# A transformer block with routed experts on one Trainium2 core: the closing stage by pairs of tiles, the experts' loops written out, two pieces of the shared expert in other banks

## The chip, the cores and the metric

The kernel is one program on one core of a Trainium2 chip. The core has five engines with queues of their own: TensorE (PE in the profile; PEld is its weight load, PEldq and PEq its sequencer), VectorE (DVE), ScalarE (ACT), GpSimd (POOL) and SyncE (SP, which here only issues transfers). They wait for one another through semaphores. The metric is the time of one execution on the device in microseconds (us), lower is better.

## The reference

The input x has 4 sequences of 512 tokens, 256 wide. Everything is float32.

```python
mod = silu(c) @ wmod                       # six vectors for each of the 4 sequences
h = layernorm(x) * (1 + ca) + sa
x = x + ga * attention(h)                  # 16 heads of 16, softmax over 512 keys, times wo
h = layernorm(x) * (1 + cb) + sb
logits = h @ gate_w.T                      # 32 experts, 4 are chosen for a token
out = sigmoid(h @ shared_gate) * (silu(h @ sg.T) * (h @ su.T)) @ sd.T
for e in range(32):                        # an expert: 256 -> 96 (gate and up) -> 256
    out += comb[:, e] * (silu(h @ gate_e.T) * (h @ up_e.T)) @ down_e.T
x = x + gb * out
```

comb holds a token's four normalised router weights and is 0 for the other experts. So 4 x 512 x 4 = 8192 (token, expert) pairs are computed.

## The kernel before, in words

The instructions of every engine are written by hand, engine by engine; no scheduler moves them. The functions have the same names in the blocks of several engines, and a semaphore joins them.

**Attention.** For each sequence in turn: normalise, project, scores, exponentials, values, output projection. Between the matrix products of attention TensorE does the projections of the next sequence and the router of the one before. GpSimd scatters the rows of each sequence into the table `dispatched` in memory, sorted by expert (`dispatch`, L541).

**The shared expert's pieces (class Finish, `finish`).** When attention ends, TensorE computes 30 pieces of the shared expert, two matrix products of 128x512 each (L972; SG is a gate, SU an up-projection) or eight of 128x256 (L966; SD, the down-projection). Piece n lies in bank `2 + n % 4` of a list of six; numbers 2 to 5 of that list are the banks 0 to 3 of PSUM. A bank is claimed when VectorE (or ScalarE) has freed its last piece; VectorE's `shared` reads the pieces in the same order (L1436 for SG behind ScalarE's tanh L652, L1445 for SU, L1448 and L1458 for SD). The last two pieces, 28 and 29, are the gates SG0 and SG1 of the last sequence. `CHAIN` and the `if n == ...` lines in the `finish` of TensorE and VectorE put the last sequence's router between the pieces: output projection behind piece 1, transposes and logits behind 6 and 7, ranks behind 10. VectorE works out the table of tiles (`tile_table`, L1392 to L1415) behind piece 12; TensorE turns it into a row (`table`, L952) behind piece 15, and VectorE packs it (`pack_table`, L1420 to L1427) behind piece 15 too.

**The experts.** The table has 96 tiles of 128 rows, each of one expert, taken in 48 pairs, one pair a slot (r is the slot's number modulo 8, q the slot). SyncE reads a tile's place from the table and loads its rows into one of 8 buffers of `xe` (L457). TensorE's slot q is, from `slots`: `turn_rows` (4 transposes of pair q, L1092, into bank 0 or 1), `widen` (up-projection of pair q-1, 4 products, L1106, into bank 2 or 3), `turn_hidden` (2 transposes of q-2, L1117), `narrow` (down-projection of q-3, 2 products, L1127). The profile counts each float32 product as two matrix instructions. Which expert's weights they use comes from `experts`: a word of the table holds four expert numbers and is read into registers (`value_load`, L1082). `slots` keeps the words that it has read in `es`, and `es` is new for each call, that is for each 8 slots:

```python
def known(r):
    w = r // 2
    if w not in es:
        es[w] = experts(XP // 2 * i + w)
    return es[w][2 * (r % 2):2 * (r % 2) + 2]
```

The first slot of a call asks for the words of pairs q-1, q and q-3, the others for one new word in two slots.
VectorE copies the transposed rows to `xeT` (tile oT, L1579) and multiplies gate, up and router weight (L1586, L1588); ScalarE computes silu (L743) and copies the hidden rows (L760) and the results (L752, to `y_sb`). GpSimd scatters the results into `results`, two indirect transfers a slot (L561). A buffer of `xe` is loaded anew when the results of its pair have landed (semaphores `y_out`). On every engine the first 8 slots are written out and the rest is a hardware loop of 5 turns (on GpSimd 6 turns) of 8 slots; the last three steps of the pipeline follow it as straight code.

**The closing stage.** After the experts TensorE computes ten last pieces of the shared expert (class Late). SyncE loads the results back, 16 tiles of 128 tokens x 4 results x 256 (`comb`, L472). For a tile, VectorE adds the four results with one 512-wide and one 256-wide addition (L1618, L1619), multiplies by the gate vector (L1620) and adds to x (L1622). For the tiles in `BY_PE`, (4, 6, 8, 10, 12, 14), TensorE adds the four results with an identity matrix instead (L1177) and VectorE multiplies out of PSUM (L1614) and adds (L1622). `cuts` says ahead of which tile VectorE takes the late pieces. ScalarE stores each tile when it is done (L783).

## Time and profile before

| what | value |
|---|---|
| timed runs | 596.38 us (median of 3; 596.19, 596.38, 599.55) |
| the profiled execution | 599.47 us; its span, first to last instruction, is 597.7 us |
| busy, whole span | TensorE 560.9 us (94%), weight load 308.7 (52%), VectorE 374.9 (63%), ScalarE 255.3 (43%), GpSimd 206.1 (34%) |
| matrix instructions | 3102 products, 3103 weight loads |
| granted clock of TensorE | 0.979 on average; 1.00 from 172 to 570 us |
| queue that fetches TensorE's code (q8) | 21 packets, 0.34 MB |
| experts' stage | 403 to 550 us |
| closing stage | 550 to 597.7 us |

The profile is of one execution, with the time of each instruction. "Busy" is time in which an engine computes; waits, branches, register steps and the issue of transfers are not busy. In a timeline several instructions of one kind are merged (x4), and the bracket behind a row says how long the engine was idle ahead of it and what ended that ("issue" is an idle time that nothing in the profile explains). 0.24 us of idle between TensorE's weight loads is their normal pace beside long products.

### The profile page before, as it was taken

To read this page: it belongs to the slowest core of one execution; us is meant where nothing else is said; L and a number is where in the kernel's file an instruction comes from. 1 tells how busy PE (TensorE), PEld (TensorE's weight loads), DVE (VectorE), ACT (ScalarE), POOL (GpSimd) and SP (SyncE) were. 2 spreads that over 40 slices of the span, in tenths; PEclk is the share of its full clock that TensorE was granted. 3 is DMA by queue.
4 is the path that set the end of the run, shared out by engine and by line. 5 is a ranking of instruction groups with operands and counts; after the bars stand their busy time and mean duration, and the time that the engine had idled before them with its cause. 6 is when DMAs were issued, how large, how long until landed. Compare 5 with 4: busy or idle time off the path is not lost.

```text
span 597.7 us, 10693 instructions
## 1 busy us (share of the span) xinstructions
PE 560.9 (94%) x3102; PEld 308.7 (52%) x3103; DVE 374.9 (63%) x888; ACT 255.3 (43%) x519; POOL 206.1 (34%) x268
## 2 busy tenths in 40 slices
PE   4989999999999999999999998989998999999983
PEld 3443323233333333333343455638887898988572
DVE  6375577778679786798856469545343443442588
ACT  3112635664866648555568240123333343444000
POOL 6200000000020751207533663722665666667200
PEclk9975999999999999999999999999999999999998
DMA  6133117100221222212100688433544655540592
GB/s 228 40 110 123 27 34 218 34 7 16 68 49 37 80 82 77 44 35 82 62 1 29 222 255 249 136 91 107 157 146 137 180 161 159 166 125 18 209 404 91
DMA packets 44119, 67.18 MB, mean 112 GB/s; under 512 B 9499, under 2 KB 32420, under 8 KB 43692
## 3 DMA queue, kind: packets, MB, share of 16 engines
q1 hardware_dynamic: 31984, 45.62, 26.5%
q0 software_dynamic: 7680, 16.87, 8.1%
q10 hardware_dynamic: 4416, 4.20, 2.1%
q8 instruction: 21, 0.34, 0.3%
q14 instruction: 18, 0.15, 0.1%
HBM read 38.93 MB, written 27.51 MB: 111 GB/s over the span
## 4 chain that ended last, share of the span: by engine, by line
PE 83%; DVE 9%; DMA 2%; issue 2%; SPq 2%; ACT 1%; POOL 0%; ACTq 0%; DVEq 0%; POOLq 0%
PE ps L875 23%; PE ps L888 11%; PE ps L1106 9%; PE ps L972 8%; PE ps L1127 6%; PE ps L824 5%; PE ps L966 4%; PE ps L1092 3%; PE ps L846 3%; PE ps L833 3%; PE ps L901 3%; DVE max_q L1217 2%; PE ps L1117 2%; PE ps L810 2%; PE ps L931 1%
## 5 line engine op out<-in xcount | busy, mean ns | idle before, releaser
L1217 DVE TENSOR_REDUCE max_q<-ps 128x1 f32<-128x512 f32 x256 | 163.7, 684 | 73.6 <-PE ps L846 71.7
L703 ACT ACTIVATE probs<-ps 128x512 f32<-128x512 f32 x256 | 138.0, 596 | 102.1 <-PE ps L875 101.8
L846 PE MATMUL ps<-k_rows,q_rows 31*128 31x512 f32 x512 | 150.1, 681 | 1.1 <-DMA k_rows<-qk_raw 1.1
L875 PE MATMUL ps<-q_rows,k_rows 32*128 32x512 f32 x512 | 146.4, 650 | 0.9 <-DVE max_q L1217 0.9
L561 POOL DMA_INDIRECT results<-y_sb,dest x96 | 94.9, 988 | 70.3 <-ACT y_sb L752 35.2
L875 PEld LDWEIGHTS ps<-q_rows,k_rows 32*128 32x128 f32 x512 | 41.8, 186 | 70.6 <-ACT probs L703 51.1
L1106 PE MATMUL ps<-up_sb,oT 128*128 x384 | 70.8, 327 | 0.9 <-issue 0.7
L888 PE MATMUL ps<-probs,v_ext 128*32 128x512 f32 x512 | 68.2, 605 | 1.1 <-ACT probs L703 1.1
L1106 PEld LDWEIGHTS ps<-up_sb,oT 128*128 128x128 f32 x384 | 61.3, 190 | 1.9 <-issue 1.8
L1579 DVE COPY oT<-ps 128x512 f32<-128x512 f32 x48 | 33.1, 691 | 32.8 <-PE ps L1092 32.8
L1127 PE MATMUL ps<-down_sb,e_hidT 96*128 x192 | 49.8, 382 | 4.0 <-ACT e_hidT L760 4.0
L846 PEld LDWEIGHTS ps<-k_rows,q_rows 31*128 31x128 f32 x512 | 45.6, 193 | 9.8 <-DVE max_q L1217 3.9
L514 POOL TENSOR_TENSOR rstd<-veps,mhalf 128x4 f32<-128x4 f32 x4 | 4.1, 1036 | 133.1 <-DVE veps L1299 131.4
L1586 DVE CAST dest<-xe 128x2 int32<-128x2 f32 x48 | 15.0, 313 | 49.2 <-ACT e_silu L743 45.8
L743 ACT ACTIVATE e_silu<-ps 128x192 f32<-128x192 f32 x48 | 15.8, 330 | 59.5 <-PE ps L1106 59.5
L752 ACT ACTIVATE y_sb<-ps 128x512 f32<-128x512 f32 x48 | 28.7, 597 | 29.4 <-PE ps L1127 26.6
L652 ACT ACTIVATE sh_tanh<-ps 128x512 f32<-128x512 f32 x16 | 9.5, 596 | 68.8 <-PE ps L972 68.8
L1127 PEld LDWEIGHTS ps<-down_sb,e_hidT 96*128 96x128 f32 x192 | 32.6, 190 | 8.0 <-issue 5.4
L888 PEld LDWEIGHTS ps<-probs,v_ext 128*32 128x32 f32 x512 | 10.1, 108 | 50.6 <-issue 34.1
L541 POOL DMA_INDIRECT dispatched<-h_even,slot_i x32 | 31.4, 982 | 9.5 <-POOL h_even L540 9.5
L541 POOL DMA_INDIRECT dispatched<-h_odd,slot_i x32 | 31.3, 978 | 9.1 <-POOL h_odd L540 9.1
L1092 PE MATMUL ps<-ident,xe 128*128 128x128 f32 x192 | 29.1, 273 | 3.5 <-issue 2.0
(181 smaller groups left out, 681.9 us busy)
## 6 DMA issues: line engine op xcount, KB each, us to landing
xe<-dispatched SPq DMA_DIRECT2D x96, 129.0 KB, 2.1
comb<-results SPq DMA_DIRECT2D x16, 512.0 KB, 10.6
up_sb<-in_up SPq DMA_DIRECT2D x12, 512.0 KB, 4.7
dispatched<-pad_rows SPq DMA_DIRECT2D x33, 129.0 KB, 4.0
down_sb<-in_down SPq DMA_DIRECT2D x4, 768.0 KB, 6.7
x<-in_x ACTq DMA_DIRECT2D x4, 512.0 KB, 4.8
q_rows<-qk_raw SPq DMA_DIRECT2D x64, 32.0 KB, 1.9
k_rows<-qk_raw SPq DMA_DIRECT2D x64, 32.0 KB, 1.9
```

The source lines that it names most:

```text
L541: pool.indirect_dma_start(out=xs, out_offset=bass.IndirectOffsetOnAxis(ap=slot_i[:, TOPK * j + k:TOPK * j + k + 1], axis=0), in_=h2[p % 2] ...
L561: pool.indirect_dma_start(out=yk, out_offset=bass.IndirectOffsetOnAxis(ap=dest[:, n:n + 1], axis=0), in_=y_sb[:, n % (2 * YP), :], in_offs ...
L703: act.activation(probs[:, u % 8, :], ps[:, st_bank(t.b, g, u), :], ACT.Exp).then_inc(exp_done, 1)
L846: pe.matmul(ps[:, banks[u % len(banks)], :], q_rows[32 * i:32 * i + ONE, b % 2, g, qt * P:(qt + 1) * P], k_rows[32 * i:32 * i + ONE, b % 2 ...
L875: pe.matmul(ps[:, st_bank(b, g, n), :], k_rows[32 * i:32 * i + 32, b % 2, g, kt * P:(kt + 1) * P], q_rows[32 * i:32 * i + 32, b % 2, g, :] ...
L888: mm = pe.matmul(ps[32 * i:32 * i + 32, O, :], v_ext[:, b % 2, kt, head(g, i), :], probs[:, (4 * kt + i) % 8, :], start=(kt == 0), stop=(k ...
L972: mm = pe.matmul(bank, w[:, k, c * P:(c + 1) * P], h2_columns(s, k), start=(k == 0), stop=(k == KD - 1))
L1092: mm = pe.transpose(ps[:, r % 2, (2 * half + k) * P:(2 * half + k + 1) * P], xe[:, 2 * r + half, k * P:(k + 1) * P], ident[:, :])
L1106: mm = pe.matmul(ps[:, 2 + r % 2, 2 * DM * half:2 * DM * (half + 1)], xeT[:, r % 2, (2 * half + k) * P:(2 * half + k + 1) * P], up_sb[:, b ...
L1127: mm = pe.matmul(ps[:, 6 + r % 2, half * D:(half + 1) * D], e_hidT[:, r % 2, half * P:(half + 1) * P], down_sb[:, bass.ds(es[half] * D, D) ...
L1217: dve.tensor_reduce(max_q[:, g % 2, qt, i:i + 1], ps[:, banks[(16 * g + n) % len(banks)], :], AXX, ALU.max).then_inc(max_done, 1)
L1579: dve.tensor_copy(xeT[:, r % 2, :], ps[:, r % 2, :]).then_inc(t_done, 1)
```

## The change

1. **Table.** `CHAIN` and both `finish` functions move TensorE's `table` and VectorE's `pack_table` from behind piece 15 to behind piece 17. `tile_table` stays behind piece 12.
2. **Banks.** Piece n of Finish lies in bank `2 + (n + 2) % 4`, so every piece moves by two banks. The last two are now in banks 2 and 3, and pieces 26 and 27 in banks 0 and 1.
3. **Loops.** The hardware loops of the experts on all five engines become Python loops: the same slots, written out, with constants where registers were.
4. **Closing stage.** VectorE's loop goes over 8 pairs of tiles with operations twice as wide (the gate vector repeated by a stride of 0), `BY_PE` is (6, 10, 14) and means pairs, TensorE sums two tiles into the halves of one bank, `cuts` has 2 in place of 1, and ScalarE stores 8 pairs.

```diff
--- before.py
+++ after.py
@@ -30,7 +30,7 @@
 YP = 4
 CR = 8
 WP = 6
-BY_PE = (4, 6, 8, 10, 12, 14)
+BY_PE = (6, 10, 14)
 
 
 class Steps:
@@ -119,7 +119,7 @@
 class Finish(Turn):
 
 
-    CHAIN = {1: ("WO0", "WO1"), 6: ("HT0", "HT1"), 7: ("LOG",), 10: ("RANK", "CNT"), 15: ("TAB",)}
+    CHAIN = {1: ("WO0", "WO1"), 6: ("HT0", "HT1"), 7: ("LOG",), 10: ("RANK", "CNT"), 17: ("TAB",)}
 
     def __init__(self, b, used):
         super().__init__(b, {"finish"}, used)
@@ -132,7 +132,7 @@
         self.shared += [f"SG0@{B - 1}", f"SG1@{B - 1}"]
         chain = 0
         for n, name in enumerate(self.shared):
-            self.take(name, 2 + n % 4, used)
+            self.take(name, 2 + (n + 2) % 4, used)
             for own in self.CHAIN.get(n, ()):
                 self.take(own, chain % 2, used)
                 chain += 1
@@ -460,7 +460,7 @@
                 if r == XP - 1:
                     written(sp, fin, f"SU3@{B - 2}")
                 load_pair(r, r)
-            with sp.Fori(1, PAIRS // XP, 1) as i:
+            for i in range(1, PAIRS // XP):
                 for r in range(XP):
 
                     sp.wait_ge(y_out[r % YP], 32 * (XP // YP * (i - 1) + r // YP + 1))
@@ -552,7 +552,7 @@
             scale_and_shift(fin)
             dispatch(fin)
 
-            with pool.Fori(0, PAIRS // XP, 1) as i:
+            for i in range(0, PAIRS // XP):
                 for r in range(XP):
                     pool.wait_ge(y_done, XP * i + r + 1)
                     apart(pool)
@@ -770,18 +770,19 @@
 
             for r in range(XP):
                 slot(0, r, r, r)
-            with act.Fori(1, PAIRS // XP, 1) as i:
+            for i in range(1, PAIRS // XP):
                 for r in range(XP):
                     slot(i, XP * i + r, r, XP)
             for r in range(3):
                 slot(PAIRS // XP, PAIRS + r, r, XP, r)
             for c in (2, 3):
                 tanh_gate(B - 1, c)
-            for t in range(NT):
-                act.wait_ge(x3_done, t + 1)
+            for t in range(0, NT, 2):
+                act.wait_ge(x3_done, t // 2 + 1)
                 b, j = divmod(t, TJ)
-                act.dma_start(out[b, j * P:(j + 1) * P, :], x[:, t * D:(t + 1) * D]).then_inc(stored, 16)
-            act.wait_ge(stored, 16 * NT)
+                act.dma_start(out[b, j * P:(j + 2) * P, :].rearrange("(j p) d -> p j d", p=P),
+                              x[:, t * D:(t + 2) * D].rearrange("p (j d) -> p j d", d=D)).then_inc(stored, 16)
+            act.wait_ge(stored, 8 * NT)
 
         @block.tensor
         def _(pe):
@@ -1047,7 +1048,7 @@
                     if n == 10:
                         ranks(t)
                         counts(t)
-                    if n == 15:
+                    if n == 17:
                         table(t)
 
             for k in range(KD):
@@ -1154,7 +1155,7 @@
                         narrow(q - 3, r - 3, known(r - 3))
 
             slots(0, range(XP), None, True)
-            with pe.Fori(1, PAIRS // XP, 1) as i:
+            for i in range(1, PAIRS // XP):
                 slots(i, range(XP), XP, True)
             slots(PAIRS // XP, range(3), XP, False)
 
@@ -1169,12 +1170,14 @@
             for c in range(2):
                 shared(f"SD{c}@{B - 1}")
             for n, t in enumerate(BY_PE):
-                pe.wait_ge(comb_ld[t], 16)
                 if n >= 2:
 
                     pe.wait_ge(prod_s, n - 1)
-                for k in range(TOPK):
-                    mm = pe.matmul(ps[:, n % 2, 0:D], ident[:, :], comb[:, t, k * D:(k + 1) * D], start=(k == 0), stop=(k == TOPK - 1))
+                for half in range(2):
+                    pe.wait_ge(comb_ld[t + half], 16)
+                    for k in range(TOPK):
+                        mm = pe.matmul(ps[:, n % 2, half * D:(half + 1) * D], ident[:, :], comb[:, t + half, k * D:(k + 1) * D],
+                                       start=(k == 0), stop=(k == TOPK - 1))
                 mm.then_inc(sum_full, 1)
 
         @block.vector
@@ -1553,7 +1556,7 @@
                         slots_out(t)
                     if n == 12:
                         tile_table(t)
-                    if n == 15:
+                    if n == 17:
                         pack_table(t)
 
             statistics(TJ, NT)
@@ -1595,30 +1598,31 @@
                 columns_out(r, r)
                 if r:
                     gated(r - 1, r - 1)
-            with dve.Fori(1, PAIRS // XP, 1) as i:
+            for i in range(1, PAIRS // XP):
                 for r in range(XP):
                     columns_out(XP * i + r, r)
                     gated(XP * i + r - 1, (r - 1) % XP)
             gated(PAIRS - 1, XP - 1)
 
-            cuts = {0: (0, 6), 1: (6, 8), 4: (8, 9), 6: (9, 10)}
-            for t in range(NT):
+            cuts = {0: (0, 6), 2: (6, 8), 4: (8, 9), 6: (9, 10)}
+            for t in range(0, NT, 2):
                 for name in late.shared[slice(*cuts.get(t, (0, 0)))]:
                     shared(name)
-                four = comb[:, t, :]
-                one = four[:, 0:D]
-                scale = mod_b[:, (3 * (t // TJ) + 2) * D:(3 * (t // TJ) + 3) * D]
+                four = comb[:, t:t + 2, :]
+                one = four[:, :, 0:D]
+                scale = mod_b[:, (3 * (t // TJ) + 2) * D:(3 * (t // TJ) + 3) * D].unsqueeze(1).to_broadcast([P, 2, D])
                 if t in BY_PE:
                     n = BY_PE.index(t)
                     dve.wait_ge(sum_full, n + 1)
-                    dve.tensor_tensor(one, ps[:, n % 2, 0:D], scale, ALU.mult).then_inc(prod_s, 1)
+                    dve.tensor_tensor(one, ps[:, n % 2, :].rearrange("p (j d) -> p j d", d=D), scale, ALU.mult).then_inc(prod_s, 1)
                     dve.wait_ge(prod_s, n + 1)
                 else:
-                    dve.wait_ge(comb_ld[t], 16)
-                    st.then(dve.tensor_tensor(four[:, 0:2 * D], four[:, 0:2 * D], four[:, 2 * D:4 * D], ALU.add))
-                    st.then(dve.tensor_tensor(one, one, four[:, D:2 * D], ALU.add))
+                    for half in range(2):
+                        dve.wait_ge(comb_ld[t + half], 16)
+                    st.then(dve.tensor_tensor(four[:, :, 0:2 * D], four[:, :, 0:2 * D], four[:, :, 2 * D:4 * D], ALU.add))
+                    st.then(dve.tensor_tensor(one, one, four[:, :, D:2 * D], ALU.add))
                     st.then(dve.tensor_tensor(one, one, scale, ALU.mult))
-                rows = x[:, t * D:(t + 1) * D]
+                rows = x[:, t * D:(t + 2) * D].rearrange("p (j d) -> p j d", d=D)
                 dve.tensor_tensor(rows, rows, one, ALU.add).then_inc(x3_done, 1)
```

What stands on TensorE where the experts' stage begins, from the last gate piece on. Before (miscN_free is what VectorE's or ScalarE's reading of a bank signals; misc2 and misc3 are the banks 0 and 1):

```order
L972 MATMUL ps<-h2T_late,sgate_sb 128x512 [waits misc3_free]
L972 MATMUL ps<-h2T_late,sgate_sb 128x512
L1092 MATMUL ps<-ident,xe 128x128 [waits up_ld0,up_ld1,misc3_free,tab_s,misc2_free,xe_ld0,misc1_free,misc0_free]
L1092 MATMUL ps<-ident,xe 128x128 x3
L1082 TENSOR_LOAD tab
L1082 ISA x2
L1092 MATMUL ps<-ident,xe 128x128 [waits xe_ld1]
L1092 MATMUL ps<-ident,xe 128x128 x3
L1106 REGISTER_ALU [waits misc5_free,misc4_free,t_done]
```

and now:

```order
L973 MATMUL ps<-h2T_late,sgate_sb 128x512 [waits misc5_free]
L973 MATMUL ps<-h2T_late,sgate_sb 128x512
L1093 MATMUL ps<-ident,xe 128x128 [waits up_ld0,up_ld1,misc3_free,tab_s,misc2_free,xe_ld0,misc1_free,misc0_free]
L1093 MATMUL ps<-ident,xe 128x128 x3
L1083 TENSOR_LOAD tab
L1083 ISA x2
L1093 MATMUL ps<-ident,xe 128x128 [waits xe_ld1]
L1093 MATMUL ps<-ident,xe 128x128 x3
L1107 REGISTER_ALU [waits misc5_free,misc4_free,t_done]
```

The instructions and their waits are the same; the gate piece ahead of them now lies in the bank that the up-projection waits for, no longer in the one that the transposes wait for.

```order
L1157 UNCONDITIONAL_BRANCH
L1157 ISA
L320 ISA [waits xe_ld0]
L1092 MATMUL ps<-ident,xe 128x128 [waits t_done]
L1092 MATMUL ps<-ident,xe 128x128 x3
L1082 ISA
L1082 TENSOR_LOAD tab
L1082 ISA x2
L320 REGISTER_ALU [waits t_done]
L1106 REGISTER_ALU [waits hid_s]
```

and now:

```order
L1093 MATMUL ps<-ident,xe 128x128 [waits t_done,xe_ld0]
L1093 MATMUL ps<-ident,xe 128x128 x3
L1083 TENSOR_LOAD tab
L1083 ISA x2
L1107 REGISTER_ALU [waits hid_s,t_done]
L1107 REGISTER_ALU
```

The wait for the loaded rows moves from a register step of its own to the first transpose, and the steps that compute the read's address and the waits' values are gone. The read of the table stays. Two more reads follow within the slot, before and now.

What stands on VectorE in the closing stage between the last four up and gate pieces. Before:

```order
L1436 SCALAR_TENSOR_TENSOR sh_tanh<-sh_tanh,ps 128x512
L1445 TENSOR_TENSOR sh_hidT<-sh_tanh,ps 128x512
L1618 TENSOR_TENSOR comb<-comb 128x512
L1619 TENSOR_TENSOR comb<-comb 128x256
L1620 TENSOR_TENSOR comb<-comb,mod_b 128x256
L1622 TENSOR_TENSOR x<-x,comb 128x256
L1436 SCALAR_TENSOR_TENSOR sh_tanh<-sh_tanh,ps 128x512
L1445 TENSOR_TENSOR sh_hidT<-sh_tanh,ps 128x512
```

and now:

```order
L1439 SCALAR_TENSOR_TENSOR sh_tanh<-sh_tanh,ps 128x512
L1448 TENSOR_TENSOR sh_hidT<-sh_tanh,ps 128x512
L1622 TENSOR_TENSOR comb<-comb 128x2x512
L1623 TENSOR_TENSOR comb<-comb 128x2x256
L1624 TENSOR_TENSOR comb<-comb,mod_b 128x2x256
L1626 TENSOR_TENSOR x<-x,comb 128x512
L1439 SCALAR_TENSOR_TENSOR sh_tanh<-sh_tanh,ps 128x512
L1448 TENSOR_TENSOR sh_hidT<-sh_tanh,ps 128x512
```

The last gate and up piece now stand behind two tiles instead of one.

## Rows read from the trace of the kernel before

**Rows 1.** Busy us by stage (length, five engines), clock, DMA share, GB/s.
```profile
50.00:172.00 122.00, 121.96 (x747) 41.27 (x747) 83.68 (x154) 70.64 (x134) 5.68 (x5) 0.97 0.21 57
...
423.00:545.00 122.00, 115.55 (x718) 104.71 (x717) 51.80 (x159) 48.14 (x120) 78.46 (x80) 1.00 0.51 147
...
570.00:598.00 28.00, 16.37 (x73) 13.20 (x71) 22.72 (x51) 0.00 (x0) 0.00 (x0) 0.92 0.60 232
```

**Rows 2.** Timeline around the table: start, length, what [idle before <-releaser].
```profile
373.46 0.69 DVE L1445 TENSOR_TENSOR sh_hidT<-sh_tanh,ps 128x512 f32<-128x512 f32 x1
373.60 0.60 PE L952 MATMUL ps<-ident,tcol 128*1 128x128 f32 x4 [1.56 <-DVE tcol L1415]
```

**Rows 3.** Timeline where the experts' stage begins.
```profile
402.63 0.69 DVE L1436 SCALAR_TENSOR_TENSOR sh_tanh<-sh_tanh,ps 128x512 f32<-128x512 f32 x1 [1.03 <-ACT sh_tanh L652]
...
403.64 0.63 PE L1092 MATMUL ps<-ident,xe 128*128 128x128 f32 x4 [1.74 <-issue]
404.30 0.69 DVE L1579 COPY oT<-ps 128x512 f32<-128x512 f32 x1 [0.98 <-PE ps L1092]
...
405.24 1.56 PE L1106 MATMUL ps<-up_sb,oT 128*128 x8
```

**Rows 4.** TensorE timeline, transposes that open slots 3, 8, 9, 13, 16, 47.
```profile
408.60 0.60 PE L1092 MATMUL ps<-ident,xe 128*128 128x128 f32 x4
...
422.72 0.60 PE L1092 MATMUL ps<-ident,xe 128*128 128x128 f32 x4
...
427.36 0.60 PE L1092 MATMUL ps<-ident,xe 128*128 128x128 f32 x4
...
439.89 0.66 PE L1092 MATMUL ps<-ident,xe 128*128 128x128 f32 x4 [1.06 <-DMA xe<-dispatched]
...
448.98 0.65 PE L1092 MATMUL ps<-ident,xe 128*128 128x128 f32 x4 [0.39 <-DMA xe<-dispatched]
...
542.44 0.60 PE L1092 MATMUL ps<-ident,xe 128*128 128x128 f32 x4
```

**Rows 5.** Table reads, 495 to 503 us; the late down-projection of slot 32.
```profile
L1082 PEldq TENSOR_LOAD <-tab x3: 301/301/309, 497.2 to 499.8; - x3
...
500.80 0.73 PEld L1127 LDWEIGHTS ps<-down_sb,e_hidT 96*128 96x128 f32 x4 [0.99 <-issue]
```

**Rows 6.** Table reads, 541 to 547 us; a down-projection behind the loop.
```profile
L1082 PEldq TENSOR_LOAD <-tab x2: 302/317/332, 543.2 to 545.4; - x2
...
546.79 1.03 PE L1127 MATMUL ps<-down_sb,e_hidT 96*128 x4
```

**Rows 7.** Groups of the closing stage: busy us, mean ns, idle before.
```profile
L1618 DVE TENSOR_TENSOR comb<-comb 128x512 f32<-128x512 f32 x10 | 6.8, 683 | 0.0
...
L1622 DVE TENSOR_TENSOR x<-x,comb 128x256 f32<-128x256 f32 x16 | 6.8, 425 | 0.5
...
L1614 DVE TENSOR_TENSOR comb<-ps,mod_b 128x256 f32<-128x256 f32 x6 | 2.5, 419 | 1.6 <-PE ps L1177 1.6
```

**Rows 8.** VectorE timeline at the end; how long stores take to land.
```profile
592.70 0.41 DVE L1614 TENSOR_TENSOR comb<-ps,mod_b 128x256 f32<-128x256 f32 x1
...
593.49 0.68 DVE L1618 TENSOR_TENSOR comb<-comb 128x512 f32<-128x512 f32 x1
...
595.13 0.42 DVE L1622 TENSOR_TENSOR x<-x,comb 128x256 f32<-128x256 f32 x1
...
DMA to landing us min/median/max: 1.7/1.7/7.1
```

**Rows 9.** Timeline: scatters of results 0 and 5, re-loads that wait for them.
```profile
413.10 0.99 POOL L561 DMA_INDIRECT results<-y_sb,dest  x1 [20.88 <-ACT y_sb L752]
...
418.92 0.34 SPq L457 DMA_DIRECT2D xe<-dispatched  x1
...
430.40 0.98 POOL L561 DMA_INDIRECT results<-y_sb,dest  x1 [0.30 <-issue]
...
436.36 1.55 SPq L457 DMA_DIRECT2D xe<-dispatched  x2
```

## The prediction

> **What bounds the kernel now.** I read the page's slices first (TensorE's digit is 9 nearly throughout), then the busy time by stage [rows 1]. Three kinds of stretch come out of it. In the attention stage TensorE is busy 121.96 of 122 us; nothing in the change touches it. In the experts' stage it is busy 115.55 of 122 us, so about 6.5 us are holes. In the closing stage TensorE is busy 16.37 of 28 us and VectorE 22.72: there VectorE sets the end. The page's chain of waits agrees: it runs along TensorE until about 575 us, and then along VectorE's additions of result tiles. So every microsecond of a TensorE hole before that point is worth one, and after it only VectorE's queue counts. I then looked for each hole with the timeline.
>
> **Table two pieces later.** Before, TensorE stops for 1.56 us ahead of the table's small products, because VectorE finishes the table's column (L1415) only then [rows 2]. After, pieces 16 and 17 of the shared expert go first. Piece 16 can start at once. Piece 17 needs the bank of piece 13, which VectorE reads right behind the table arithmetic, 373.46 + 0.69 = 374.15 us [rows 2]. One piece is 1.72 us (two pieces take 3.44 in the order shown), so piece 16 ends at 372.04 + 1.72 = 373.76 and a wait of 0.4 stays. Gain 1.1 to 1.2. The table itself is ready some 1.5 us later, near 378; its first users are the loads of expert rows at 394.9 and TensorE at 403, so that costs nothing. What hid the 1.2 us otherwise? Nothing: from 374 to 401.9 TensorE runs without a hole, and the expert rows that it needs next have landed (first pair at about 398).
>
> **Last gate pieces in other banks.** The experts' first transposes write banks 0 and 1. Before, the last two gate pieces sit there, and the transposes wait until VectorE has read the last one: 402.63 + 0.69 = 403.32, start 403.64, copy 404.30, first up-projection 405.24 [rows 3]. After, banks 0 and 1 were left by pieces 26 and 27, free since about 398, so the transposes follow TensorE's last gate piece directly. The bound moves to VectorE's queue: the copy stands behind that gate piece, at 403.36 instead of 404.30, and the up-projection waits for the copy. Gain 0.9. Both parts together: 1.2 + 0.9 = 2.1 us. The later pairs of rows have landed in time even 2.1 us earlier (they are issued every 1.1 us, needed every 2.8). Bounds: 0.9 if the first wait only moves to piece 17, 2.6 if neither leaves a rest.
>
> **Experts' loops written out.** A group of four transposes marks each slot [rows 4]. From slot 3 (408.60) to slot 8 (422.72) a slot takes 2.824 us, and the matrix work alone fills that. From slot 3 to slot 47 are 44 slots, 44 x 2.825 = 124.3 us; the rows give 542.44 - 408.60 = 133.84. Excess 9.5 us. Of it two waits for re-loaded rows: slot 13 came 439.89 - 427.36 - 4 x 2.825 = 1.23 late, slot 16 448.98 - 439.89 - 3 x 2.825 = 0.62 late. The other 7.7 stand at the five places where a turn of the loop begins (427.36 - 422.72 - 2.825 = 1.8 at the first, 1.5 on average).
> What happens there: TensorE's sequencer reads expert numbers from the table three times within a slot, elsewhere once in two slots. Each read is 0.30 us plus its checks, about 0.85 in all [rows 5]; the third ends so late that the down-projection starts 0.99 us late. The changed kernel has all three reads at the same places, so the reads do not go. What goes is what stands ahead of them: in the loop the wait for the rows (xe_ld0) is one of the sequencer's own instructions, and the reads cannot start before the rows have landed; written out, that wait rides on the transpose and the sequencer passes it. It also loses one address step per read and three steps that compute wait values.
> How much? The code behind the loop, already straight, reads the table in the same dense way, and no idle time stands ahead of its matrix work [rows 6]. There it is two reads, not three, and no transposes. I take the holes as gone whole: 7.7 us. The other bound: the sequencer still waits as late as now and saves only the removed steps, seven of about 0.1 us at each place, 0.72 x 5 = 3.6 us. I am nearer to the first because in straight slots the sequencer is seen 1.5 to 2 us ahead, and three reads need 2.6 of the 3.2 us to the down-projection. The two waits for rows (1.85) I leave as they are. ScalarE, VectorE, GpSimd and SyncE lose steps too; none of them bounds here (GpSimd needs 2 x 1.29 of 2.825 us a slot), so that is worth nothing by itself.
>
> **Closing stage by pairs.** The same tiles stay with VectorE (10) and with TensorE's sums (6). A 512-wide operation takes 683 ns, a 256-wide one 425 [rows 7], so 256 more elements cost 258 ns and 167 are fixed. A 1024-wide one was never run here; by that line it takes 1.20 us. It could be read in two parts at 2 x 0.68 = 1.37; I take 1.20, since the slope is what the engine did from 256 to 512. Now a tile of VectorE's own takes 1.64 us for three operations (593.49 to 595.13) [rows 8] and 0.335 for the last, which overlaps the next tile: 1.975, a pair 3.95. As a pair: 1.20 + 0.68 + 0.68 + 0.11 between them + 0.59 = 3.27. Five pairs save 5 x 0.68 = 3.4. A TensorE tile takes 0.79 (592.70 to 593.49), a pair 1.58; after, 0.68 + 0.04 + 0.59 = 1.31; three pairs save 0.8. Together 4.2. The wait of 1.6 us for TensorE's first sum [rows 7] shrinks: the pair that TensorE sums first is tiles 6 and 7, which VectorE reaches at about 579.6 us of the old clock. TensorE starts them 1.2 later than before (its shared down-projection waits for the piece that VectorE now reads behind a whole pair), at 576.5, and needs 3.5, so 0.4 stay, and another 0.4 ahead of that down-projection. Waits 1.6 to 0.9: gain 0.7. Result tiles land well ahead of their use. The last store carries 256 KB in place of 128 KB, which now takes 1.7 us to land [rows 8]; it can cost 0 to 1.7 more, I take 0.5, as a store here is mostly fixed time. Net 4.2 + 0.7 - 0.5 = 4.4 us.
>
> By the Trainium skill, page Perfetto Trace Analysis, section Optimizing Scalar/DVE Operations, a VectorE operation on SBUF has about 60 ns of overhead in engine-busy time, half of what a profile shows. An estimate by that page: 26 fewer operations x 0.06 = 1.6 in place of 4.2. The rows of starts (three dependent operations in 1.64 us) speak for the larger figure in this kernel.
>
> **The sum.** 2.1 + 7.7 + 4.4 = 14.2 us off the profiled execution, whose time is 599.47 us (span 597.7): 585.3. That execution stood 3.1 above the median of the timed runs, 596.38. Part of the 3.1 may be in the very holes that go, so against the median I count 14.2 - 0.8 = 13.4: 583.0 us. About 1% (6 us) is what a measurement of this kernel tells from no change.
>
> **Rivals.**
> 1. The reads stay in the way. For: they stay in the program at the same places, and each is 0.85 us during which nothing is issued. Against: the straight code of rows 6. Gain in the loops 3.6 in place of 7.7: 583.0 + 4.1 = 587.1.
> 2. Re-loading rows becomes the bound. A slot's rows are re-loaded when its last result has landed. Slot 3 starts at 408.60, its result's scatters at 413.10, 4.5 later, and take 2.29; then the landing L; then two loads 1.2 apart and 2.1 to land. Against five slots, 14.1 us, L may be 4.06. Seen are 418.92 - 415.39 = 3.5, and once 436.36 - 431.38 = 5.0 [rows 9], which made slot 13 wait. If two landings in each of five turns exceed by 0.9, 9 us less the 1.85 there now is 7.2: 590.2. Against: the 5.0 is the only one of that size I found; the later landings are 2.4 to 3.3.
> 3. VectorE's fixed part is mostly hidden already, so pairs save 1.6 instead of 4.2: 585.6. Against it rows 8.
> 4. Slower: straight code has to be fetched from memory, loop code hardly. The experts' TensorE code grows by four copies of a turn, by the page's 6205 matrix instructions in 21 packets some 5 to 8 packets more. If TensorE ran dry at each, it would decide from 14.2 / 7 = 2 us a packet; at 3 us a packet the time is 583.0 + 21 = 604. Against: the attention stage is straight code, 1494 matrix instructions in 122 us, without a hole [rows 1], and slots 3 to 8 are straight too.
> By the Trainium skill, page Runtime: NRT & Kernel Launch, section Instruction fetch mechanics, crossing a block of code is mostly hidden and a taken branch is what breaks the prefetch. The rows on straight code agree; the branch's own part in the 7.7 us no row here shows.
>
> **How the numbers follow.** Forecast 0.60, rival 1 0.17, rival 2 0.10, rival 3 0.06, rival 4 0.04, and 0.03 for a time near or above 590.4 through several small losses. The range: low 579.5, where the waits for rows go too (1.85) and the last store costs nothing; high 589.5, which takes in rivals 1 and 3 and half of rival 2. Faster by over 1% means under 590.4: 0.90. Within 1%: 0.07. Slower: 0.03.
>
> **What would show it.** Right: slots of 2.82 us through all 48, with no hole behind slots 8, 16, 24, 32 and 40; the first up-projection 2 us earlier; the 1024-wide addition near 1.20 us; VectorE's additions end 4.9 us sooner after the last piece. Rival 1 shows as idle ahead of the down-projection (0.3 to 1.1 us) in those five slots; rival 2 as waits of the transposes for the row loads; rival 4 as idle of TensorE at any place with no releaser. The forecast is wrong if the experts' stage is not shorter by at least 5 us.

## The result and the profile after

The kernel before takes 596.84 us (median of 8 runs beside the changed kernel), the changed kernel 591.23 us. The ratio is 0.9886, 95% interval 0.9856 to 0.9916: 6.8 us less by the ratio, between 5.0 and 8.6, where 13.4 had been forecast, and over the high end of the range (589.5). The profiled execution of the changed kernel takes 589.51 us, its span is 587.7 us and its mean granted clock 0.982.

| stage, from the two traces | before | after | difference | forecast |
|---|---|---|---|---|
| start to the last product with values of attention (code unchanged) | 332.51 | 330.31 | -2.2 | 0 |
| from there to the transposes of slot 3 | 76.09 | 73.96 | -2.1 | -2.1 |
| slot 3 to slot 47 | 133.84 | 132.52 | -1.3 | -7.7 |
| slot 47 to the end of the span | 55.27 | 50.95 | -4.3 | -4.4 |

The first line is no effect of the change: eleven traces of kernels with this attention code, taken where the kernel before runs in about 597 us, have that product's start between 330.3 and 333.1 us. The other three sum to 7.8 us, within the interval of 5.0 to 8.6. Two of three terms came out as forecast. The third did not.

The timeline of the changed kernel around the table, which answers to [rows 2]:

```profile
371.86 1.98 PE L973 MATMUL ps<-h2T,sup_sb 128*128 128x512 f32 x4 [0.45 <-DVE sh_hidT L1448]
...
373.77 0.60 PE L953 MATMUL ps<-ident,tcol 128*1 128x128 f32 x4
```

The wait of 1.56 us ahead of the small products is gone, and 0.45 us stands ahead of piece 17 (forecast 0.4).
The timeline where the experts' stage begins, which answers to [rows 3]:

```profile
398.48 1.04 PE L1093 MATMUL ps<-ident,xe 128*128 128x128 f32 x8
...
399.38 0.69 DVE L1439 SCALAR_TENSOR_TENSOR sh_tanh<-sh_tanh,ps 128x512 f32<-128x512 f32 x1 [1.03 <-ACT sh_tanh L652]
399.98 1.28 DVE L1582 COPY oT<-ps 128x512 f32<-128x512 f32 x2
...
400.91 1.56 PE L1107 MATMUL ps<-up_sb,oT 128*128 x8 [1.40 <-DVE oT L1582]
```

The transposes (eight merged: slots 0 and 1) follow the gate piece at once, and the copies stand right behind VectorE's reading of that piece. Before, the copy followed the reading's start by 1.67 us (402.63 to 404.30), now by 0.60: the bound is VectorE's queue, as said.

The closing stage. The groups of VectorE there (line, shapes, count, busy us, mean ns, idle before):

```profile
L1622 DVE TENSOR_TENSOR comb<-comb 128x1024 f32<-128x1024 f32 x5 | 6.1, 1220 | 0.0
L1626 DVE TENSOR_TENSOR x<-x,comb 128x512 f32<-128x512 f32 x8 | 5.5, 692 | 0.3
L1624 DVE TENSOR_TENSOR comb<-comb,mod_b 128x512 f32<-128x512 f32 x5 | 3.5, 692 | 0.2
L1623 DVE TENSOR_TENSOR comb<-comb 128x512 f32<-128x512 f32 x5 | 3.5, 692 | 0.2
...
L1617 DVE TENSOR_TENSOR comb<-ps,mod_b 128x512 f32<-128x512 f32 x3 | 2.1, 687 | 0.3 <-PE ps L1179 0.3
```

The addition over 1024 elements takes 1.22 us (forecast 1.20), and the waits for TensorE's first sum are 0.3 us in all; [rows 7] has 1.6 for one.

Now the experts' stage. The TensorE timeline of the changed kernel at slot 32, and the group of the table reads in the same stretch (ns of one at least/in the middle/at most, first and last start):

```profile
489.43 1.03 PE L1128 MATMUL ps<-down_sb,e_hidT 96*128 x4
491.46 0.66 PE L1093 MATMUL ps<-ident,xe 128*128 128x128 f32 x4 [1.00 <-DMA xe<-dispatched]
492.55 1.56 PE L1107 MATMUL ps<-up_sb,oT 128*128 x8 [0.43 <-issue]
493.94 0.38 PE L1118 MATMUL ps<-ident,e_hid 128*96 128x128 f32 x2
495.05 1.13 PE L1128 MATMUL ps<-down_sb,e_hidT 96*128 x4 [0.72 <-ACT e_hidT L760]
```

```profile
L1083 PEldq TENSOR_LOAD <-tab x3: 301/308/344, 491.5 to 494.0; - x3
```

The hole ahead of the down-projection is still there: 0.72 us of idle on TensorE's row here, where [rows 5] has 0.99 us on the weight load's row. (Its releaser is given as ScalarE's copy, L760, but that was done long before: the weight load of the down-projection waits for the third read.) In the view of waits the five holes of this kind sum to 4.0 us before and 3.6 us after (us in all, times, longest), first before, then after:

```profile
PE ps L1127 <- ACT e_hidT L760: 4.0, 5, 0.9
```

```profile
PE ps L1128 <- ACT e_hidT L760: 3.6, 5, 0.7
```

And the first read starts with the transposes, at 491.46, when the rows that they waited for had landed (the last at 491.41). The prediction had the sequencer pass that wait. Here the read does not.

The slots are 2.82 us apart in 37 of the 44 steps. The five first slots of groups take 4.52, 3.79, 3.83, 4.55 and 4.05 us, 6.6 us over 5 x 2.825; before it was 7.7. Two waits for rows, ahead of slots 8 and 32, make the step to these slots 1.6 us longer (before 1.85).

### The profile page after: what moved, and what is told of

It is laid out like the page before. It is cut to its first block, busy times and chain, and to the rows that moved or that the text cites. A ratio compares the mean times of both kernels' runs of the same rounds, so it can differ in the third digit from the quotient of the medians.

```text
span 587.7 us, 10308 instructions
## 1 busy us (share of the span) xinstructions
PE 556.5 (95%) x3102; PEld 308.3 (52%) x3102; DVE 371.3 (63%) x862; ACT 255.0 (43%) x519; POOL 206.6 (35%) x268
## 4 chain that ended last, share of the span: by engine, by line
PE 81%; DVE 9%; issue 3%; DMA 3%; ACT 1%; POOL 1%; SPq 1%; POOLq 0%; ACTq 0%; DVEq 0%
PE ps L876 23%; PE ps L889 11%; PE ps L1107 8%; PE ps L973 7%; PE ps L1128 6%; PE ps L825 5%; PE ps L967 4%; PE ps L834 3%; PE ps L847 3%; PE ps L1093 3%; PE ps L902 3%; DVE max_q L1220 2%; PE ps L811 2%; DMA results<-y_sb,dest 1%; PE ps L932 1%
## 5 line engine op out<-in xcount | busy, mean ns | idle before, releaser
L967 PE MATMUL ps<-sdown_sb,sh_hidT 128*128 128x256 f32 x128 | 28.6, 380 | 2.1 <-issue 2.1
```

What stands on the lines that cost most here:

```text
L967: mm = pe.matmul(bank[:, (j % 2) * D:(j % 2 + 1) * D], sh_hidT[:, f, j * P:(j + 1) * P], sdown_sb[:, f, :], start=(f == 0), stop=(f == 3))
```

## The experiments

**Theory A.** The hole is made by the three reads of a group's first slot, in the straight code as in the loop. They can't start before the slot's rows have landed, since the transpose that waits for them stands ahead. **Rivals.** B: rows that land late are the bound. C: the place itself costs (a branch, code that is fetched, another engine's steps).

The kernels ran in four groups, each beside the kernel before on one chip, and one kernel ran once more by itself in between, for a look. In the first two groups, eight kernels, everything took some 50 us longer; they have a section of their own. The second measurements are the ones to go by.

### Words once read stay known

```diff
+            es = {}
             def slots(i, rs, begun, more):
-                es = {}
                 def known(r):
-                    w = r // 2
+                    w = XP // 2 * i + r // 2
                     if w not in es:
-                        es[w] = experts(XP // 2 * i + w)
+                        es[w] = experts(w)
```

> The changed kernel with one difference: a word of the table that TensorE has read stays known in the next group of eight slots, so the first slot of a group reads one word instead of three (12 reads fewer in all). Theory A (three reads in a row on TensorE's sequencer, which cannot begin before the rows of that slot have landed, make the hole): the slots 8, 16, 24, 32 and 40 take 2.8 to 3.0 us instead of 3.8 to 4.5, the 6.6 us of excess at those five places fall below 1.5, time 591.2 - 5.5 = 585.7. Theory B (the rows of these slots come late and would be the bound without the reads): the reads go but the transposes then wait for the re-loaded rows, the stage shortens by under 2 us, 589.5 or more. Theory C (the place costs time by itself, by fetching of code or by another engine): slots 8, 16, 24, 32, 40 stay near 4 us, 591.

> The kernel of the first group again (words once read stay known, one read instead of three in a group's first slot), for a look. The chip of the first eight runs shows stretches in which a step of a sequencer takes 0.7 us, which the first two profiles don't have, and they cover the slots. If this run has none of them (the kernel before at 594 to 601 us): theory A wants the slots 8, 16, 24, 32 and 40 at 2.82 to 3.0 us where no row wait falls on them, slot 3 to slot 47 at 124.3 to 128 us (132.5 in the changed kernel), 585.7. Theory B wants waits of the transposes for the re-loaded rows of over 1 us in those slots. If it has them, again 634 to 644 us.

> Words once read stay known, timed beside the changed kernel on one chip. The look gave 585.7 us, slot 3 to slot 47 in 126.9 us against 132.5 in the changed kernel. Theory A: 5.0 to 6.0 us under the changed kernel of this group, ratio to the kernel before 0.977 to 0.981. If the look was a lucky execution, under 3 us.

Measured: 639.38 us against 649.93 in the first group (ratio 0.9844, 0.9788 to 0.9899); in the look 585.68 us against 598.80 (one run each); timed, 585.03 us against 595.88 of the kernel before and 589.65 of the changed kernel on that chip (0.981, 0.976 to 0.986). That is 4.6 us under the changed kernel, a little less than the 5.0 to 6.0 expected. The TensorE timeline of the timed kernel's profile at slot 24, with the one read that is left:

```profile
467.27 0.60 PE L1093 MATMUL ps<-ident,xe 128*128 128x128 f32 x4
467.71 1.47 PE L1107 MATMUL ps<-up_sb,oT 128*128 x8
469.01 0.38 PE L1118 MATMUL ps<-ident,e_hid 128*96 128x128 f32 x2
469.23 1.03 PE L1128 MATMUL ps<-down_sb,e_hidT 96*128 x4
470.10 0.66 PE L1093 MATMUL ps<-ident,xe 128*128 128x128 f32 x4
```

```profile
L1083 PEldq TENSOR_LOAD <-tab x1: 392/392/392, 467.7 to 467.7; - x1
```

No hole: the slot takes 2.83 us. Slot 3 to slot 47 takes 126.91 us in the look and 127.43 in the timed kernel's profile, 4.8 to 5.6 less than the changed kernel's 132.52 and 132.23. B falls, but not wholly: of the 6.6 us, about 5 to 5.5 stay gone and the rest comes back as waits of the transposes for rows (three in the timed kernel's profile, 1.8 us of idle in all, one of them, 0.6 us, behind slot 32). C falls: the places are the same, the code is as straight, and in the look's profile the five first slots take 2.82 to 2.92 us. No other kernel of this study has a lower median.

### One read more

```diff
                     if more:
                         turn_rows(i, q, r)
+                    if more and i and r == 0:
+                        experts(XP // 2 * i)
```

> The changed kernel with one read of the table more (its value unused) in the first slot of the four later groups and of the first of them, five in all, right behind the transposes. Theory A: each adds a read of 0.30 us with its checks, 0.85 us, to the hole ahead of the down-projection or of the up-projection: +0.85 x 5 = 4.3 us, 595.5. Theories B and C: the reads lie beside matrix work that waits for something else, within 1 us of the changed kernel, 591.2 to 592.2.

> The changed kernel with one more read of the table in each group's first slot. Theory A: those slots grow by 0.85 us each, slot 3 to slot 47 by 4.3 us to 136.8, time 4.3 us over the changed kernel. If the place costs time for another reason, within 1 us of the changed kernel.

Measured in the first group 641.66 us, ratio 0.988 (0.984 to 0.9919), where the changed kernel has 0.9865 in the second. On the other chip: 595.94 us against 589.65 of the changed kernel, 6.3 us more by the medians, where 4.3 were expected. The two profiled executions differ by 7.2 us: 3.2 in the experts' stage (slot 3 to slot 47 in 135.41 us), 2.3 ahead of slot 3, and 1.7 in the closing stage, where TensorE's granted clock stood at its lower level (0.50, 1.2 GHz) for 3.4 us, from 569.55 us on, as it did not in the changed kernel's. So the reads' own part is the 3.2 us, 0.6 us for each and not 0.85. A hole stands in all five slots with and without the added read, so little of it can be hidden; but it follows the read ahead of it at once, with no products' steps between, in three of the five slots by 0.65 to 0.73 us. From a group's first read to the down-projection it is 4.28 to 4.91 us, in the changed kernel of this group 3.53 to 3.81. The rows of slot 24:

```profile
471.63 0.60 PE L1093 MATMUL ps<-ident,xe 128*128 128x128 f32 x4
472.46 1.56 PE L1107 MATMUL ps<-up_sb,oT 128*128 x8 [0.23 <-issue]
473.92 0.40 PE L1118 MATMUL ps<-ident,e_hid 128*96 128x128 f32 x2
474.99 1.13 PE L1128 MATMUL ps<-down_sb,e_hidT 96*128 x4 [0.67 <-ACT e_hidT L760]
```

### The reads ahead of the wait

```diff
+                    if more and i and r == 0:
+                        known(-1), known(0), known(-3)
                     if more:
                         turn_rows(i, q, r)
```

> The changed kernel with the three reads of a group's first slot ahead of that slot's transposes instead of among its products; same reads, same number. Theory A: they no longer stand behind the wait for the rows, so the first of them begins about 1.6 us ahead of the landing and the third ends about 516.1 on the changed kernel's clock, where now it ends at 518.4; the hole of 1.2 us moves ahead of the transposes and shrinks to 0.5 to 0.7: gain 0.5 to 0.7 a group, 2.5 to 3.5 us, 588.2. Rival: the read waits for what the engine does, not for the rows, and begins as late as now: the time is 591 or, as all three come ahead of the transposes, up to 2 us a group more, 601.

> The changed kernel with the three reads of a group's first slot ahead of that slot's transposes. Theory A (the read waits for the rows only because the waiting transpose stands ahead of it): the first read begins over 0.5 us ahead of the rows' landing, the hole moves ahead of the transposes, and a first slot takes 3.3 to 3.7 us instead of 3.8 to 4.5: 2 to 3 us under the changed kernel. Rival (the read waits for the engine to be idle, wherever it stands): no gain, or up to 2 us a group more.

Measured: 639.16 us in the first group (0.9837, 0.9791 to 0.9883); in the last 586.07 us against 597.67 (0.9817, 0.9764 to 0.9871), by the ratios 4 us under the changed kernel, more than the 2 to 3 expected. (The intervals of the two ratios touch; slot 3 to slot 47 in the profiles is what tells them apart.) This is the run that tests the failed step itself: the same reads in the same number, only on the other side of the wait. Slot 32 of its profile, timeline and reads:

```profile
489.10 1.03 PE L1128 MATMUL ps<-down_sb,e_hidT 96*128 x4
490.31 0.66 PE L1093 MATMUL ps<-ident,xe 128*128 128x128 f32 x4 [0.18 <-DMA xe<-dispatched]
490.80 1.48 PE L1107 MATMUL ps<-up_sb,oT 128*128 x8
492.12 0.38 PE L1118 MATMUL ps<-ident,e_hid 128*96 128x128 f32 x2
492.34 1.03 PE L1128 MATMUL ps<-down_sb,e_hidT 96*128 x4
```

```profile
L1083 PEldq TENSOR_LOAD <-tab x3: 294/295/338, 465.2 to 466.5; - x3
...
L1083 PEldq TENSOR_LOAD <-tab x3: 295/301/304, 487.7 to 489.0; - x3
```

Here too the transposes wait for rows. But the reads ran at 487.7 to 489.0, while the rows were still on their way, beside the products of the slot before. Three reads cost nearly nothing there: the hole of 1.0 to 1.7 us is down to 0.5 or less, ahead of the transposes, and slot 3 to slot 47 takes 127.27 us, 5 less than in the changed kernel's two profiles. In all five groups the first read starts ahead of the last landing of the slot's rows, by 0.5 to 2.8 us. So it was the place of the reads behind the wait, and not their number, that made the hole.

### The loops written out, alone

```diff
-            with pe.Fori(1, PAIRS // XP, 1) as i:
+            for i in range(1, PAIRS // XP):
```

and so on the other four engines, in the kernel before.

> The kernel before with one part of the change alone: the experts' loops written out on all five engines. Theory A: it saves only the steps around the reads, 1 to 1.5 us: 596.8 - 1.3 = 595.5. The theory of the prediction (written out, the sequencer passes the wait and the holes go): 596.8 - 7.7 = 589.1. If fetching straight code costs: above 598.

> The kernel before with the loops written out alone. Theory A: slot 3 to slot 47 takes 1 to 2 us less than in the kernel before and stays over 131 us, 596.8 - 1.5 = 595.3, ratio 0.9975. The theory of the prediction: 126 us, ratio 0.987.

Measured: 0.9935 (0.9905 to 0.9966) in the first group; later 596.53 us against 595.88, ratio 0.9986 (0.9945 to 1.0028), from 3.3 us less to 1.7 more. Slot 3 to slot 47 takes 131.21 us in its profile. Three executions with the loops unchanged have 133.84, 131.40 and 133.74; three with all of them written out 131.21, 132.52 and 132.23. So the step is worth about 1 us, not 7.7, and the traces scatter by more than that.

This profile also shows why the hole varies. At slot 40, timeline and reads:

```profile
517.76 0.60 PE L1092 MATMUL ps<-ident,xe 128*128 128x128 f32 x4
518.20 1.47 PE L1106 MATMUL ps<-up_sb,oT 128*128 x8
519.50 0.38 PE L1117 MATMUL ps<-ident,e_hid 128*96 128x128 f32 x2
519.72 1.04 PE L1127 MATMUL ps<-down_sb,e_hidT 96*128 x4
520.60 0.60 PE L1092 MATMUL ps<-ident,xe 128*128 128x128 f32 x4
```

```profile
L1082 PEldq TENSOR_LOAD <-tab x3: 297/299/307, 516.1 to 518.6; - x3
```

Three reads and no hole: the rows of this slot had landed by 516.06, 1.7 us ahead of the transposes, and the reads had begun at once. So a read does pass transposes that the engine has not begun; what it does not pass is their wait while that is unmet. Where the first read starts with the transposes, as at slot 32 of the changed kernel (491.5 and 491.46), the slot is 1.7 us too long. Between them, slot 24 of the changed kernel, the first read at 465.9, 0.8 us ahead of the transposes (466.68), is 1.0 too long. In the 15 first slots of three profiles with the loops written out (the changed kernel's two and this one) the hole is 1.7 to 2.1 us less the time by which the rows were early.

### One read a slot later, the loops kept

```diff
-                    if more:
+                    if more and (r or begun is None):
                         known(r)
```

in the kernel before: the first slot of a turn reads two words, the second one reads the third.

> The kernel before, loops kept, with the second of the three reads moved from the turn's first slot into its second slot, where there is none. Theory A: the first slots lose a read's 0.85 us and the second slots hide it: slot 3 to slot 47 in 129 to 131 us (133.8 before), 592.5 to 594, ratio 0.993 to 0.996. If the hole belongs to the branch of the loop or to the number of reads in a turn: no change, ratio 0.998 to 1.002.

Measured: 594.42 us against 597.67, ratio 0.9951 (0.9922 to 0.998), slot 3 to slot 47 in 130.40 us. Moving a read helps in the loop, without writing anything out. The second slots took 3.17 to 3.18 us, so a part of the read shows there, ahead of the up-projection: the gain is 2.9 us by the ratio (1.2 to 4.7) and not 4.3, five times 0.85. The interval's upper end touches the rival's 0.998, and one profile with the loop untouched has 131.40; what tells is the way from a turn's first read to the down-projection, 2.96 to 3.06 us with two reads and 3.63 to 3.91 in the kernel before, with three.

### The closing stage alone, and the table with the banks alone

The edits are those of parts 4, and 1 and 2, of the diff.

> The kernel before with the closing stage by pairs alone. Both traces gave 4.3 us between slot 47 and the end of the span: 596.8 - 4.3 = 592.5, ratio 0.993. The prediction had 4.4. If VectorE's fixed part was mostly hidden (rival 3), 1.8: ratio 0.997.

> The kernel before with the closing stage by pairs alone. If the 4.3 us seen between slot 47 and the end of the span in the changed kernel's trace are the closing stage's own: slot 47 to the end in 50.5 to 51.5 us (55.3 before), about 592, ratio 0.993. If fixed parts of VectorE were hidden: 53.5 us, ratio 0.997.

Measured: 0.997 (0.9939 to 1.0) in the second group; in the last 593.87 us against 597.67, ratio 0.9933 (0.9903 to 0.9963), 4.0 us less. In its profile slot 47 to the end is 52.6 us and not under 51.5: TensorE's granted clock stood at its lower level (0.50) for 3.4 us there, from 569.4 us on, 1.7 us of product time. The part that doesn't hang on that clock, from TensorE's first sum to the end of the span, is 17.01 us, as in the changed kernel, against 22.58 before: 5.6 less; ahead of it the shared pieces end 1.25 us later, as said in the prediction (1.2).

> The kernel before with the table two pieces later and the pieces moved by two banks, nothing else. Both traces gave 2.1 us at slot 3 (prediction 2.1): 596.8 - 2.1 = 594.7, ratio 0.9965. If the earlier start is only waited for later (the rows' re-loads set the pace of the experts), ratio 1.000 and slot 47 is no earlier.

> The kernel before with the table two pieces later and the banks moved, nothing else. If the 2.1 us are kept to the end: from the last product with values of attention to slot 3 in 74.0 us (76.1 before), ratio 0.9965. If the experts' stage gives them back in row waits: the same 74.0 us, but slot 3 to slot 47 longer by 2 us, ratio 1.000.

Measured: 0.9983 (0.9951 to 1.0015) in the second group; in the last 596.08 us against 597.67, ratio 0.9969 (0.9938 to 1.0000), 1.9 us less. From the last product with values to slot 3 it is 74.02 us against 76.09, and slot 3 to slot 47 takes 133.74: nothing is given back. The parts multiply to 0.9933 x 0.9969 x 0.9986 = 0.9888; the whole change measured 0.9886. Each part is known to 0.3 or 0.4%, so part of so close an agreement is chance.

### The first two groups, where this could not be seen

> The kernel before itself, unchanged, for a trace of it from the chip on which this group of runs is made, since the first four kernels ran on a chip where the kernel before takes 649.9 us and not 596.8. If the extra 53 us are stalls of one kind (ScalarE, VectorE or TensorE standing with all that they wait for already there), they stand in this trace too, in the loops as in the straight code; if they come from straight code alone, the experts' loops of this kernel show none, and slots are 2.82 us apart there apart from the five turns and the row waits. On a chip like that of the first profiles the time is 594 to 601 us.

> The changed kernel unchanged, beside the kernel before on the chip of this group. If the gain is what it was, the ratio is 0.986 to 0.992. If straight code costs on this chip, the ratio is nearer to 1.

> The changed kernel as the measure for the other three of this group: ratio to the kernel before 0.9885, slot 3 to slot 47 in 132 to 133 us, the first slots of the groups at 3.8 to 4.5 us.

In the first two groups the kernel before takes 649.93 and 649.58 us, the changed one 640.3 (0.9865, 0.9823 to 0.9907). In the third group the changed one takes 589.65 (0.9887, 0.9839 to 0.9935): the same ratio within the intervals. It need not be the chip: the record numbers the chips of the first two groups 7 and 9, and the last group, in which the kernel before takes 597.67 us, ran on number 9 again, an hour later. SyncE's reads of the table (line 456, steps of its sequencer) between 500 and 560 us in the changed kernel, first in the second group, then in the first profile:

```profile
L456 SPq TENSOR_LOAD <-tab x33: 4/268/704, 500.6 to 557.3; - x33
L456 SPq FUSED_REGOPS  x33: 3/152/701, 500.9 to 557.6; - x33
L456 SPq SEQ_ASSERT  x33: 3/18/700, 501.4 to 557.8; - x33
```

```profile
L456 SPq TENSOR_LOAD <-tab x22: 264/268/686, 502.3 to 533.0; - x22
L456 SPq FUSED_REGOPS  x22: 152/152/159, 502.6 to 533.3; - x22
L456 SPq SEQ_ASSERT  x22: 18/18/18, 502.8 to 533.5; - x22
```

A step of 18 ns takes 700 there at times; the middle value is unchanged. These steps come in stretches. The waits of the changed kernel in the second group from 425 to 590 us (us in all, times, longest):

```profile
ACT e_silu L743 <- remote: 37.2, 8, 6.7
...
PE ps L1118 <- DVE e_hid L1591: 8.2, 5, 2.9
```

ScalarE stands 37.2 us with no releaser that the profile knows ("remote"; the kernel has one core), which the first profile has nowhere, and TensorE then waits for the hidden rows. From slot 3 to slot 47 the five kernels with loops written out take 154.7 to 156.4 us there, with one, three or four reads alike, and the three with loops 157.7 to 162.2. So these groups could not decide between A and C. The stretches stand in the loops as in the straight code. What slows the steps stays open; no run here varied it.

## Why the prediction was wrong

- **Table and banks: right.** 2.1 us forecast, 2.1 in the trace, 1.9 by the ratio of that part alone. The rest of 0.4 ahead of piece 17 was seen as 0.45.
- **Closing stage: right.** 4.4 forecast, 4.3 in the trace, 4.0 by the ratio alone. The parts came out too, so this is not luck: the line through the 256-wide and 512-wide operations gave 1.20 us for 1024 elements, measured 1.22; TensorE's idle time ahead of the shared down-projection grew from 0.83 to 2.10 us (forecast 1.2 more); from the last addition's end to the end of the span it is 2.59 us, before 2.15 (forecast 0.5 more). The sum by the 60 ns an operation of the Trainium skill, page Perfetto Trace Analysis, section Optimizing Scalar/DVE Operations (1.6 us), was too small. The rows say why: a 256-wide addition starts 0.46 us after the one whose result it needs (594.21 to 594.67) and only 0.35 after one that it does not need (577.58 to 577.93), and most of the operations here stand in such chains.
- **Experts' loops: the failed step.** The prediction says "written out, that wait rides on the transpose and the sequencer passes it", and with it "I take the holes as gone whole: 7.7 us". Measured: 1.3 in the traces, 0.8 (-1.7 to 3.3) by the ratio of that part alone. In the changed kernel's trace the first read of each group starts 0.05 us behind the last landing of the slot's rows, in all five places, also where the engine begins the transposes only 1 us later; in the loop it was 0.27 to 0.31. So the sequencer is ahead, as the prediction had seen, but only up to a read behind an unmet wait. From that read to the down-projection's weight load it is 3.63 to 3.91 us before (3.64 at [rows 5], 497.16 to 500.80) and 3.55 to 3.76 after (3.58 from 491.46).
- **The bound below it was wrong as well.** I counted seven removed steps of 0.1 us in each place, 3.6 us. Four went: the step that waited for the rows and the address step of each read. The three that compute a wait's value were replaced by steps that only wait. The first read comes 0.23 us sooner behind the landing, and the way from it is 0.12 us shorter in the mean: 0.35 us a place, 1.7 in all. The excess of the five slots fell by 1.1 only, since the rows were early by 0.14 us less in the mean in the trace after (0.04 to 0.98 us, before 0.13 to 1.09); that differs from execution to execution.
- **The row that misled.** The code behind the loop [rows 6] reads the table twice, with no row wait ahead. It was used as a stand-in for three reads behind such a wait.
- **Rival 1 was the right one in kind:** the reads stay in the way. Its time, 587.1, rested on the same 3.6 us and was too low: 591.23 measured.
- **Rival 2** showed only where the holes were really gone: slot 3 to slot 47 is then 2.6 to 3.1 us over its pure pace (126.9 to 127.4 against 124.3 us), and 0.8 and 1.8 us of that stand in the two profiles as idle time that ends with a landing of rows. **Rival 3** falls by the 1220 ns and the 4.0 us of the closing stage alone.
- **Rival 4 falls.** The queue that fetches TensorE's code has 28 packets instead of 21 (5 to 8 more were forecast; packets, MB, share):

```profile
q8 instruction: 28, 0.46, 0.3%
```

and no hole of TensorE between slot 3 and slot 47 is without the reads or a row wait. The Trainium skill, page Runtime: NRT & Kernel Launch, section Instruction fetch mechanics, has a taken branch break the prefetch of code where its target lies outside the two blocks at hand. Whether that held for the loop's branches no run shows. With all loops written out the time fell by 0.8 us (-1.7 to 3.3), and the steps that went account for that.

The 3.1 us by which the profiled execution of before stood over the median I had put partly into the holes (0.8). 2.2 of them were the attention stage: 332.51 us at its end, where others with that code have as little as 330.28.

## What to carry to other kernels

A read of the table into a register stood behind the unmet wait ahead of it on TensorE's queue, whether that wait was a step of its own (the loop) or rode on a matrix instruction (written out): it began 0.27 to 0.31 and 0.05 us behind the landing. A queue that is seen to be ahead of its engine is not ahead of such a wait. So put such reads ahead of the wait, or do away with them by keeping what was read (with the whole change 11 us under the kernel before here), before touching the loop around them. And a stand-in row proves something only if it has the same instructions and the same waits ahead of it.

## What the runs showed of the hardware that was not expected

- A table read of 0.30 us with its checks costs nothing when it starts early enough: three of them, begun 1.65 us ahead of the slot's transposes, left no hole, and begun with them 1.7 us. The first of them started 0.05 us behind the landing that it had to wait for, up to 1.65 us ahead of transposes that stand ahead of it in the program.
- The same kernels ran in 650 us instead of 597 in two groups (changed: 640 instead of 591), with stretches in which a step of a sequencer takes 0.7 us, in loops and in straight code. The ratio of the whole change was the same within the intervals (0.9865 and 0.9887), and so were those of its parts; that of the kernel with one read more was not (0.988, 0.984 to 0.9919, against 0.998, 0.9937 to 1.0023).
- In three of the eleven profiles from groups at 597 us TensorE's granted clock falls from 1.00 to 0.50 (from 2.4 to 1.2 GHz) for 3.4 us in the closing stage. Each time it falls 0.1 to 0.9 us after the engine took up work again behind 2.1 us without any. The way from the first load of result tiles to TensorE's first sum took 19.5 us there instead of 17.8. All seven profiles with the closing stage by pairs have these 2.1 us of idle time, since the last up and gate pieces stand behind a pair of tiles; without the pairs it is 0.83 us. The other four kept the full clock; what decides between them was not tried.
